# PSUM banks divided anew: four for the exponentials and one for the replicated u, instead of three and two

## The chip, the cores and the metric

The kernel runs on one core of a Trainium2 chip. A core has four computing engines with instruction streams of their own: PE (TensorE, matmuls), DVE (VectorE), ACT (ScalarE) and POOL (GpSimd); SP (SyncE) issues DMAs. They meet at semaphores alone. PSUM, where PE writes its results, has eight banks of 128 partitions by 512 float32. The metric is the device time of one execution in microseconds. Everything is float32.

## The reference

One transformer block with a Mamba layer (4 sequences of 2048 tokens, 256 channels) and a mixture of experts. The part that the change touches is the selective scan:

```
deltaA = exp(delta[..., None] * A)                 # 512 channels x 16 states
dBu = (delta * u)[..., None] * B[:, :, None, :]
h = dA_i * h + dBu_i                               # over the 2048 tokens
y = einsum('bdn,bn->bd', h, C_i)
```

Before it stand a layer norm, an input projection, a convolution over 4 tokens, silu, and the projections that give delta, B and C; behind it `y * silu(res)`, the output projection and the residual. Then comes the feed-forward part (shared expert, routing to one of seven experts), which the change doesn't touch.

## The kernel before

`build` runs five programs one after the other. `mamba_program` is the one that matters here: 16 chunks of T = 512 tokens. The 512 channels by 16 states of a chunk are cut into NSET = 16 *sets* of 32 channels. In a set the 128 partitions hold 32 channels x 4 state groups (NF), and NG = 4 state rows of 512 tokens lie beside each other, so a set has four scans of 128x512.

The work of a set s goes through all engines:

- PE replicates delta*u of the 32 channels to 128 partitions by a matmul with the constant `spread` into `u_ps` (L414, "u s" below). This is done for the ten sets in `OWN_SETS` (0 to 5, 8, 9, 12, 13). For the other six POOL does the product from a copy made by DMA.
- DVE multiplies that by B: `states_in`, L603, "SI s" below; its input is `u_ps`.
- ACT makes four exponentials into `dA` (L533), one PSUM bank each in a ring of ABANK banks.
- DVE runs the four scans (L616), which read `dA`.
- ACT copies the last column as state (L538, `save`), POOL multiplies by C (L694), PE sums the states (L424, `sum_states`), DVE gates the sum (L623).

Beside that the engines do groups of matrix work for the neighbouring chunks, placed by the table `plan` at a set: T (transposes), XS and RS (input projection), CV (convolution, four matmuls), XP, DT, DB (projections for delta, B, C) for chunk c+1, called "front", and OP (output projection) for chunk c-1, called "back". A group's result goes to one of two PSUM banks `bank0` and `bank1` and is read from there by ACT (or DVE). A float32 matmul shows in the trace as two matmul instructions, so u is two, XS or RS is four, CV eight.

There is no scheduler: every engine executes its `body` in program order. In ACT's body the four exponentials of set s come first, then `save` of set s-1, then the copies of the groups planned at s, then the exponentials of set s+1. In PE's body, at set s, `spread_u` for set s+2 comes first, then the groups planned at s, then a state sum. In DVE's body SI s+1 stands before the scans of set s, but where s+1 is a multiple of four it stands behind them (SI 4, SI 8, SI 12), and SI 5, SI 9, SI 13 follow at once, with only a gate (and behind SI 12 the layernorm statistics) in between. SI 0 and SI 1 stand together at the head of a chunk.

Two waits matter. ACT's exponential u (0 to 63 in the chunk) waits for scan u - ABANK to be done. PE's replication number i waits for the product number i-2 to be done, since `u_ps` has two halves used in turn.

Of the kernel before, what the change touches and what calls it, by code (L numbers as in the profile page):

```python
# [25 lines left out]
P = 128  # L26
# [4 lines left out]
T = 512  # L31
# [5 lines left out]
DS = 32  # L37
NSET = DI // DS
NF = P // DS
NG = STATE // NF  # L40
SPC = P // DS
RING = 8
ABANK = 3
NBANK = 2
EPS = 1e-5
BIG = 3.4028234e38
# [146 lines left out]
def mamba_program(nc, ins, t, bc_dram, x1_dram, wout_dram):  # L193
# [4 lines left out]
    with ExitStack() as ctx:  # L198
        sem = lambda n: ctx.enter_context(nc.semaphore(n))
        sb = lambda n, s: ctx.enter_context(nc.sbuf_tensor(n, s, F32))  # L200
        ps = lambda n, s: ctx.enter_context(nc.psum_tensor(n, s, F32))
# [4 lines left out]
        xpad, us, res = t["xpad"], sb("us", [P, 2, KI, T]), sb("res", [P, 2, KI, T])  # L206
# [4 lines left out]
        hs = sb("hs", [P, RING, NG, T])  # L211
        state = t["state"]
        banks = [ps(f"bank{i}", [P, T]) for i in range(NBANK)]
        y_ps, u_ps, dA = ps("y_ps", [P, T]), ps("u_ps", [P, 2, T]), ps("dA", [P, ABANK, T])

        x_loaded, stats_ready, rstd_step, shift_ready, xn_ready = sem("x_loaded"), sem("stats_ready"), sem("rstd_step"), sem("shift_ready"), sem("xn_ready")
        ln_step, hT_ready = sem("ln_step"), sem("hT_ready")
# [8 lines left out]
        dbu_own, dbu_shared, scan_done, state_saved, hc_ready = sem("dbu_own"), sem("dbu_shared"), sem("scan_done"), sem("state_saved"), sem("hc_ready")  # L226
# [4 lines left out]
        N_OWN, N_SHARED = len(OWN_SETS), len(SHARED_SETS)  # L231
# [14 lines left out]
        known = lambda c: isinstance(c, int)  # L246
# [28 lines left out]
        def bodies(eng, body):  # L275

            body(0, 0)
            body(1, 1)
            with eng.Fori(2, NCHUNK - 1 - CPB, CPB) as c:
                for i in range(CPB):  # L280
                    body(c + i if i else c, (2 + i) % CPB)
            body(NCHUNK - 2, 2)
            body(NCHUNK - 1, 3)
# [84 lines left out]
        @block.tensor  # L368
        def _(pe):
            def group(g, c, f, par=0):  # L370

                kind, j = g
                ps_ = take_bank(pe, g, c)
                if kind == "T":
                    if j == 0:
                        pe.wait_ge(xn_ready, f + 1)
                    for tt in range(TT):
                        last = nc.tensor.transpose(ps_[:, tt * P:(tt + 1) * P], xin[:, tt, j * P:(j + 1) * P], t["ident"][:])
                elif kind in ("XS", "RS"):
                    col = j * P + (DI if kind == "RS" else 0)  # L380
                    pe.wait_ge(hT_ready, KD * f + KD)
                    for k in range(KD):
                        last = nc.tensor.matmul(ps_[:, :], t["w_in"][:, k, col:col + P], hT[:, k, :], start=(k == 0), stop=(k == KD - 1))  # L383
                elif kind == "CV":
                    pe.wait_ge(xs_ready, KI * f + j + 1)
                    for k in range(KCONV):
                        last = nc.tensor.matmul(ps_[:, :], t["w_conv"][:, j, k, :], xpad[:, j, k:k + T], start=(k == 0), stop=(k == KCONV - 1))  # L387
                elif kind == "XP":
                    pe.wait_ge(us_ready, f + 1)
                    for k in range(KI):  # L390
                        last = nc.tensor.matmul(ps_[0:PROJ, :], t["w_x"][:, k, :], us[:, 1 - par, k, :], start=(k == 0), stop=(k == KI - 1))
                elif kind in ("DT", "DB"):
                    pe.wait_ge(xdbl_ready, f + 1)
                    last = nc.tensor.matmul(ps_[:, :], t["w_dt"][:, j * P:(j + 1) * P], xdbl[0:DT_ROWS, :], start=True, stop=True)  # L394
                elif kind == "OP":
                    pe.wait_ge(yg_ready, KI * c)
                    if j == 0:
                        pe.wait_ge(wout_loaded, 16 * ((c - 1) // CPB) + 16)
                    for h in range(2):
                        for k in range(KI):  # L400
                            tt = 2 * j + h
                            last = nc.tensor.matmul(ps_[:, h * D:(h + 1) * D], res[:, 1 - par, k, tt * P:(tt + 1) * P], t["w_out"][:, k, :],
                                                    start=(k == 0), stop=(k == KI - 1))
                last.then_inc(made[kind], 1)

            def spread_u(c, s, par):

                i = OWN_SETS.index(s)
                q, j = divmod(s, KI)
                if i == 0:  # L410
                    pe.wait_ge(du_ready, c + 1)
                if not (known(c) and c == 0 and i < 2):
                    pe.wait_ge(dbu_own, N_OWN * c + i - 1)
                nc.tensor.matmul(u_ps[:, i % 2, :], t["spread"][DS * q:DS * q + DS].rearrange("p f d -> p (f d)"), us[DS * q:DS * q + DS, par, j, :],  # L414
                                 start=True, stop=True, tile_position=(DS * q, 0)).then_inc(u_made, 1)

            def sum_states(c, j):

                pe.wait_ge(hc_ready, NSET * c + SPC * (j + 1))
                if not (known(c) and c == 0 and j == 0):  # L420
                    pe.wait_ge(yg_ready, KI * c + j)
                for g in range(NG):
                    for q in range(SPC):
                        last = nc.tensor.matmul(y_ps[DS * q:DS * q + DS, :], t["gather"][:], hs[:, (SPC * j + q) % RING, g, :],  # L424
                                                start=(g == 0), stop=(g == NG - 1), skip_group_check=True,
                                                tile_position=(0, DS * q))
                last.then_inc(y_ready, 1)

            def body(c, m):
                par = m % 2  # L430
                for s in range(NSET):
                    if s + 2 in OWN_SETS:
                        spread_u(c, s + 2, par)
                    for g in plan.get(s, []):
                        if has_front(c) if g in front else has_back(c):
                            group(g, c, c + 1, par)
                    if s == SUM_AT and has_back(c):
                        sum_states(c - 1, KI - 1)
                    if s > SPC and s % SPC == SUM_AT:
                        sum_states(c, s // SPC - 1)  # L440
                    if s + 2 >= NSET and has_front(c):
                        spread_u(c + 1, s + 2 - NSET, 1 - par)

            for g in front:
                group(g, None, 0, 1)
            spread_u(0, 0, 0)
            spread_u(0, 1, 0)
            bodies(pe, body)
            sum_states(NCHUNK - 1, KI - 1)
            for g in back:  # L450
                group(g, NCHUNK, None, 0)

        @block.scalar
        def _(act):
# [67 lines left out]
            def exps(c, s):  # L522
# [3 lines left out]
                for g in range(NG):  # L526
                    u = NG * s + g
                    if u >= ABANK:
                        act.wait_ge(scan_done, NG * NSET * c + u - ABANK + 1)
                    elif not (known(c) and c == 0):  # L530
                        last = max(v for v in range(NG * NSET) if v % ABANK == u)
                        act.wait_ge(scan_done, NG * NSET * (c - 1) + last + 1)
                    nc.scalar.activation(dA[:, u % ABANK, :], d_rep[:, q % 2, j, :], ACT.Exp, scale=t["a"][:, u:u + 1]).then_inc(da_ready, 1)  # L533

# [39 lines left out]
        def _(dve):  # L574
# [20 lines left out]
            def states_in(c, s, par):  # L595

                i = OWN_SETS.index(s)
                dve.wait_ge(u_made, N_OWN * c + i + 1)
                if s % KI == 0 and not (known(c) and c == 0 and s < RING):
                    dve.wait_ge(y_ready, SPC * c + (s - RING) // KI + 1)  # L600
                if s == 0:
                    dve.wait_ge(bc_loaded, 16 * 2 * NF * (c + 1))
                nc.vector.tensor_tensor(hs[:, s % RING], u_ps[:, i % 2, :].unsqueeze(1).to_broadcast([P, NG, T]),  # L603
                                        b_rep[:, par, :].rearrange("p (g t) -> p g t", g=NG), ALU.mult).then_inc(dbu_own, 1)

            def scan_set(c, s, m):
# [6 lines left out]
                for g in range(NG):  # L613
                    u = NG * s + g
                    dve.wait_ge(da_ready, NG * NSET * c + u + 1)
                    nc.vector.tensor_tensor_scan(hs[:, s % RING, g, :], dA[:, u % ABANK, :], hs[:, s % RING, g, :], state[:, u:u + 1] if m else 0.0,  # L616
                                                 ALU.mult, ALU.add).then_inc(scan_done, 1)
# [702 lines left out]
```

## Time and profile before

| | us |
|---|---|
| median of 3 runs | 3147.56 (3146.91 to 3148.33) |
| profiled execution, whole | 3146.25 |
| profiled execution, span from first to last instruction | 3144.5 |
| busy over the span: PE, DVE, POOL, ACT | 2277.3, 2028.9, 1981.0, 1363.8 |
| mean granted TensorE clock | 0.822 of full speed |

The `mamba_program` takes the span from about 60 to 2105 us; behind it stand the feed-forward programs, where PE is busy most of the time. The shares of busy time are means over both parts. What a change of the scan stage is worth is read from that stage's own waits: who stands still, for whom, and what is behind it in that engine's program order.

### The profile page before, as it was taken

Reading aid. Unit: us, or ns where it says so; the run is one execution under the profiler, and the core shown is the slowest. Engines: PE = TensorE matmul, PEld = TensorE weight load, DVE = VectorE, ACT = ScalarE, POOL = GpSimd, SP = SyncE. Lnnn points to the kernel's source line nnn. Section 1 sums busy time; section 2 is a strip of 40 time slices with the busy share of each in tenths; the row PEclk is TensorE's granted clock in tenths of the full one; section 3 lists DMA queues with packets and bytes.
Section 4 is the critical chain, followed back from the end, with each engine's and each line's share of the span. In section 5 each row is a group of like instructions: output and inputs, shape, how many; then the busy total and the mean of one; then the engine's idle time right before and its main releaser. Section 6 shows DMA issues by size and latency. Waiting matters only on the chain. (4 is left out here: it accounts for less than half of the span.)

```text
span 3144.5 us, 28848 instructions
## 1 busy us (share of the span) xinstructions
PE 2277.3 (72%) x7448; PEld 1051.1 (33%) x7449; DVE 2028.9 (65%) x2297; ACT 1363.8 (43%) x2182; POOL 1981.0 (63%) x816
## 2 busy tenths in 40 slices
PE   4768667686686677676867866437888960699998
PEld 3213223232232232232322322114555540366664
DVE  3488978879879788788798897943444441122222
ACT  1474655664655656646656556411222210122221
POOL 0298888888888888888898888950000006455553
PEclk8778788787787786877877877668999995899999
DMA  2333332432423243324324332424111110222221
GB/s 105 81 75 74 83 73 64 105 82 60 93 72 80 63 92 82 75 62 108 75 61 96 71 83 56 92 82 153 54 60 60 60 41 1 67 86 84 83 85 54
DMA packets 104208, 238.30 MB, mean 76 GB/s; under 512 B 18444, under 2 KB 72462, under 8 KB 91536
## 3 DMA queue, kind: packets, MB, share of 16 engines
q1 hardware_dynamic: 84112, 189.85, 25.0%
q0 software_dynamic: 14368, 36.00, 3.9%
q10 hardware_dynamic: 5600, 11.01, 0.9%
q8 instruction: 48, 0.79, 0.1%
q14 instruction: 80, 0.66, 0.1%
HBM read 106.10 MB, written 39.20 MB: 46 GB/s over the span
## 5 line engine op out<-in xcount | busy, mean ns | idle before, releaser
L694 POOL TENSOR_TENSOR hs<-hs,c_rep 128x2048 f32<-128x2048 f32 x256 | 1152.8, 4522 | 282.4 <-ACT state L538 282.4
L616 DVE TENSOR_TENSOR_SCAN hs<-dA,state,hs 128x512 f32<-128x512 f32 x768 | 917.9, 1261 | 206.4 <-ACT dA L533 206.4
L533 ACT ACTIVATE dA<-d_rep,a 128x512 f32<-128x512 f32 x1024 | 679.1, 686 | 468.9 <-DVE hs L616 459.3
L687 POOL TENSOR_TENSOR hs<-u_rep,b_rep 128x2048 f32<-128x2048 f32 x96 | 432.3, 4525 | 0.1
L603 DVE TENSOR_TENSOR hs<-u_ps,b_rep 128x2048 f32<-128x2048 f32 x160 | 362.3, 2273 | 5.5 <-PE u_ps L414 5.5
L394 PE MATMUL bank<-xdbl,w_dt 65*128 65x512 f32 x256 | 190.1, 874 | 242.0 <-DVE delta L592 232.7
L424 PE MATMUL y_ps<-hs,gather 128*32 128x512 f32 x2048 | 299.0, 736 | 60.6 <-POOL hs L694 60.5
L383 PE MATMUL bank<-xin,w_in 128*128 128x512 f32 x512 | 283.1, 693 | 75.5 <-ACT xdbl L491 47.6
L616 DVE TENSOR_TENSOR_SCAN hs<-dA,hs 128x512 f32<-128x512 f32 x256 | 290.5, 1201 | 71.9 <-ACT dA L533 71.9
L387 PE MATMUL bank<-xpad,w_conv 128*128 128x512 f32 x512 | 260.4, 662 | 96.0 <-DVE xres L630 94.5
L414 PE MATMUL u_ps<-us,spread 32*128 32x512 f32 x320 | 219.4, 781 | 109.2 <-POOL us L678 61.9
L788 POOL TENSOR_TENSOR rstd<-var,mhalf 128x4 f32<-128x4 f32 x16 | 16.1, 1007 | 410.8 <-DVE var L890 410.8
L1170 PE MATMUL z<-w1r,hT 128*128 x560 | 261.3, 610 | 2.6 <-issue 2.0
L1252 DVE TENSOR_TENSOR hid<-z,sg 128x512 f32<-128x512 f32 x70 | 48.4, 692 | 298.8 <-ACT sg L1230 298.8
L387 PEld LDWEIGHTS bank<-xpad,w_conv 128*128 128x128 f32 x512 | 105.7, 212 | 240.5 <-issue 129.7
L383 PEld LDWEIGHTS bank<-xin,w_in 128*128 128x128 f32 x512 | 101.5, 211 | 230.4 <-issue 123.9
L394 PEld LDWEIGHTS bank<-xdbl,w_dt 65*128 65x128 f32 x256 | 59.7, 258 | 353.5 <-DVE delta L592 254.3
L424 PEld LDWEIGHTS y_ps<-hs,gather 128*32 128x32 f32 x2048 | 70.0, 132 | 305.2 <-issue 210.2
L1137 POOL DMA_INDIRECT out<-outr,cur x70 | 71.2, 1016 | 143.4 <-DVE outr L1245 139.1
L486 ACT ACTIVATE us<-bank,cb 128x512 f32<-128x512 f32 x64 | 43.9, 686 | 245.8 <-PE bank L387 245.8
L414 PEld LDWEIGHTS u_ps<-us,spread 32*128 32x128 f32 x320 | 57.8, 218 | 255.3 <-issue 137.9
L1170 PEld LDWEIGHTS z<-w1r,hT 128*128 128x128 f32 x560 | 101.6, 191 | 120.7 <-issue 120.6
(170 smaller groups left out, 2862.2 us busy)
## 6 DMA issues: line engine op xcount, KB each, us to landing
d_rep<-delta SPq DMA_DIRECT2D x256, 256.0 KB, 4.3
u_rep<-us SPq DMA_DIRECT2D x192, 128.0 KB, 3.2
b_rep<-bc_rows SPq DMA_DIRECT2D x64, 256.0 KB, 4.5
c_rep<-bc_rows SPq DMA_DIRECT2D x64, 256.0 KB, 7.3
xin<-in_x SPq DMA_DIRECT2D x16, 512.0 KB, 3.6
xres<-in_x SPq DMA_DIRECT2D x16, 512.0 KB, 4.9
x<-xres SPq DMA_DIRECT2D x16, 512.0 KB, 3.2
x_sb<-x SPq DMA_DIRECT2D x16, 512.0 KB, 4.3
```

What stands on the lines that cost most here:

```text
L383: last = nc.tensor.matmul(ps_[:, :], t["w_in"][:, k, col:col + P], hT[:, k, :], start=(k == 0), stop=(k == KD - 1))
L387: last = nc.tensor.matmul(ps_[:, :], t["w_conv"][:, j, k, :], xpad[:, j, k:k + T], start=(k == 0), stop=(k == KCONV - 1))
L394: last = nc.tensor.matmul(ps_[:, :], t["w_dt"][:, j * P:(j + 1) * P], xdbl[0:DT_ROWS, :], start=True, stop=True)
L414: nc.tensor.matmul(u_ps[:, i % 2, :], t["spread"][DS * q:DS * q + DS].rearrange("p f d -> p (f d)"), us[DS * q:DS * q + DS, par, j, :], st ...
L424: last = nc.tensor.matmul(y_ps[DS * q:DS * q + DS, :], t["gather"][:], hs[:, (SPC * j + q) % RING, g, :], start=(g == 0), stop=(g == NG - ...
L533: nc.scalar.activation(dA[:, u % ABANK, :], d_rep[:, q % 2, j, :], ACT.Exp, scale=t["a"][:, u:u + 1]).then_inc(da_ready, 1)
L603: nc.vector.tensor_tensor(hs[:, s % RING], u_ps[:, i % 2, :].unsqueeze(1).to_broadcast([P, NG, T]), b_rep[:, par, :].rearrange("p (g t) -> ...
L616: nc.vector.tensor_tensor_scan(hs[:, s % RING, g, :], dA[:, u % ABANK, :], hs[:, s % RING, g, :], state[:, u:u + 1] if m else 0.0, ALU.mul ...
L687: nc.gpsimd.tensor_tensor(hs[:, s % RING], u_rep[:, q % 2, j - 2, :].unsqueeze(1).to_broadcast([P, NG, T]), b_rep[:, par, :].rearrange("p ...
L694: nc.gpsimd.tensor_tensor(hs[:, s % RING, :, :], hs[:, s % RING, :, :], c_rep[:, par, :].rearrange("p (g t) -> p g t", g=NG), ALU.mult).th ...
L1137: nc.gpsimd.indirect_dma_start(out, bass.IndirectOffsetOnAxis(cur[:, q, 2:3], 0), outr[:, q, :], None, bounds_check=BATCH * SEQ - 1, oob_i ...
L1170: last = nc.tensor.matmul(z[:, q % 2, half, :], hT[:, q % 2, i, :], t["w1r"][:, e, i, half * H:(half + 1) * H], start=(i == 0), stop=(i == ...
```

## The change

The eight PSUM banks are shared out differently. Before: two for the groups, one for `y_ps`, two for `u_ps`, three for `dA`. Now: two, one, one, four. `ABANK` becomes 4, so exponential u waits for scan u - 4. `u_ps` has one bank, so replication i waits for product i-1. The order of the instructions on PE, DVE, ACT and POOL is the same as before; only what they wait for differs (and a few register instructions of the sequencers that form the wait values).

```diff
-ABANK = 3
+ABANK = 4
...
-        y_ps, u_ps, dA = ps("y_ps", [P, T]), ps("u_ps", [P, 2, T]), ps("dA", [P, ABANK, T])
+        y_ps, u_ps, dA = ps("y_ps", [P, T]), ps("u_ps", [P, T]), ps("dA", [P, ABANK, T])
...
-                if not (known(c) and c == 0 and i < 2):
-                    pe.wait_ge(dbu_own, N_OWN * c + i - 1)
-                nc.tensor.matmul(u_ps[:, i % 2, :], t["spread"][DS * q:DS * q + DS].rearrange("p f d -> p (f d)"), us[DS * q:DS * q + DS, par, j, :],
+                if not (known(c) and c == 0 and i == 0):
+                    pe.wait_ge(dbu_own, N_OWN * c + i)
+                nc.tensor.matmul(u_ps[:], t["spread"][DS * q:DS * q + DS].rearrange("p f d -> p (f d)"), us[DS * q:DS * q + DS, par, j, :],
...
-                nc.vector.tensor_tensor(hs[:, s % RING], u_ps[:, i % 2, :].unsqueeze(1).to_broadcast([P, NG, T]),
+                nc.vector.tensor_tensor(hs[:, s % RING], u_ps[:].unsqueeze(1).to_broadcast([P, NG, T]),
```

## Rows read from the trace of the kernel before

**Rows 1.** Costliest groups: line engine op, shapes, count | busy us, mean ns | idle before

```profile
L616 DVE TENSOR_TENSOR_SCAN hs<-dA,state,hs 128x512 f32<-128x512 f32 x768 | 917.9, 1261 | 206.4 <-ACT dA L533 206.4
L533 ACT ACTIVATE dA<-d_rep,a 128x512 f32<-128x512 f32 x1024 | 679.1, 686 | 468.9 <-DVE hs L616 459.3
```

**Rows 2.** DVE's waits from 60 to 2130 us: for whom, total, times, longest

```profile
DVE hs L616 <- ACT dA L533: 278.2, 91, 8.1
...
DVE hs L603 <- PE u_ps L414: 5.5, 2, 4.9
```

**Rows 3.** Timeline of DVE, first half of a chunk: start, length, line, count [idle before]

```profile
1230.63 4.48 DVE L603 TENSOR_TENSOR hs<-u_ps,b_rep 128x2048 f32<-128x2048 f32 x2
...
1243.66 4.81 DVE L616 TENSOR_TENSOR_SCAN hs<-dA,state,hs 128x512 f32<-128x512 f32 x4 [1.66 <-ACT dA L533]
...
1250.57 9.50 DVE L616 TENSOR_TENSOR_SCAN hs<-dA,state,hs 128x512 f32<-128x512 f32 x8
1259.98 2.27 DVE L603 TENSOR_TENSOR hs<-u_ps,b_rep 128x2048 f32<-128x2048 f32 x1
1262.17 0.68 DVE L623 TENSOR_TENSOR res<-y_ps,res 128x512 f32<-128x512 f32 x1
...
1264.96 4.80 DVE L616 TENSOR_TENSOR_SCAN hs<-dA,state,hs 128x512 f32<-128x512 f32 x4
1271.62 4.81 DVE L616 TENSOR_TENSOR_SCAN hs<-dA,state,hs 128x512 f32<-128x512 f32 x4 [1.86 <-ACT dA L533]
...
1283.89 4.81 DVE L616 TENSOR_TENSOR_SCAN hs<-dA,state,hs 128x512 f32<-128x512 f32 x4 [6.87 <-ACT dA L533]
```

**Rows 4.** Timeline of DVE, sets 8 to 10 of the same chunk

```profile
1296.01 2.27 DVE L603 TENSOR_TENSOR hs<-u_ps,b_rep 128x2048 f32<-128x2048 f32 x1
...
1300.99 9.50 DVE L616 TENSOR_TENSOR_SCAN hs<-dA,state,hs 128x512 f32<-128x512 f32 x8
1315.37 4.81 DVE L616 TENSOR_TENSOR_SCAN hs<-dA,state,hs 128x512 f32<-128x512 f32 x4 [4.88 <-ACT dA L533]
```

**Rows 5.** Timeline of PE in the same chunk

```profile
1232.96 2.07 PE L414 MATMUL u_ps<-us,spread 32*128 32x512 f32 x2 [0.93 <-DVE hs L603]
...
1238.63 3.78 PE L383 MATMUL bank<-xin,w_in 128*128 128x512 f32 x4 [1.70 <-ACT xin L473]
...
1253.93 1.12 PE L414 MATMUL u_ps<-us,spread 32*128 32x512 f32 x2
1254.98 7.14 PE L387 MATMUL bank<-xpad,w_conv 128*128 128x512 f32 x16
1263.13 3.72 PE L402 MATMUL bank<-w_out,res 128*128 128x256 f32 x16 [1.01 <-DVE res L623]
...
1277.07 5.48 PE L387 MATMUL bank<-xpad,w_conv 128*128 128x512 f32 x8 [6.79 <-DVE xres L630]
...
1290.55 1.12 PE L414 MATMUL u_ps<-us,spread 32*128 32x512 f32 x2
1291.60 3.70 PE L383 MATMUL bank<-xin,w_in 128*128 128x512 f32 x8
1295.14 3.60 PE L391 MATMUL bank<-us,w_x 128*97 128x512 f32 x8
...
1303.74 3.00 PE L383 MATMUL bank<-xin,w_in 128*128 128x512 f32 x4 [3.29 <-ACT xdbl L491]
```

**Rows 6.** Timeline of ACT before the exponentials of set 10

```profile
1309.51 0.60 ACT L498 ACTIVATE delta<-bank 128x512 f32<-128x512 f32 x1 [0.44 <-PE bank L394]
...
1314.65 2.73 ACT L533 ACTIVATE dA<-d_rep,a 128x512 f32<-128x512 f32 x4
```

**Rows 7.** Timeline of DVE in the last chunk

```profile
2054.72 18.90 DVE L616 TENSOR_TENSOR_SCAN hs<-dA,state,hs 128x512 f32<-128x512 f32 x16
```

**Rows 8.** Windows: stretch, length, PE, PEld, DVE, ACT, POOL busy, PE clock, DMA, GB/s

```profile
1232.90:1236.90 4.00, 3.94 (x10) 2.06 (x10) 4.00 (x4) 0.57 (x1) 4.00 (x2) 0.50 0.89 187
...
1255.00:1262.10 7.10, 7.10 (x17) 2.93 (x16) 7.10 (x6) 2.20 (x4) 7.10 (x3) 1.00 0.54 111
```

## The prediction, made before the changed kernel was run

> **What bounds the kernel now.** I read the groups of instructions by line first. They show a scan stage that runs from about 120 to 2100 us: 1024 exponentials of 686 ns on ACT, 1024 scans on DVE, 768 of them at 1261 ns [rows 1], and on DVE too the products of L603, two in 4.48 us [rows 3]. DVE's waits come next. Over that stage DVE loses 278.2 us waiting for exponentials, in 91 waits, and only 5.5 us waiting for the replicated u [rows 2]. So the loop that sets the pace is DVE's: 16 chunks of some 122 us. Third come the timelines of DVE, PE and ACT in one chunk, from 1230.63 us. The reader should see that DVE's waits are not evenly spread. They stand before the scans of sets 1, 5, 6, 7, 10 and 11, 16 us or more in all per chunk, some of them in [rows 3, 4]. Each is behind one of the "front" groups: ACT's program has the copy of that group *before* the next set's exponentials, so a group that PE delivers late delays the scan. An example of the length of that link: PE ends XS0 at 1238.63 + 3.78 = 1242.41 and scan 1 starts at 1243.66, 1.25 us later; for CV3 it is 1277.07 + 5.48 = 1282.55 to 1283.89, 1.35 us [rows 3, 5]. A pair of u matmuls takes 2.07 us when PE has idled before it and 1.12 us when it has worked [rows 5].
>
> **What the fourth bank gives.** In set s, exponential 4 no longer needs scan 1 of its own set but the last scan of set s-1. It can start one scan (1.2 us) earlier, and so can the state copy and the group behind it. That helps only where ACT waits for a scan and not for PE. In set 0 ACT's fourth exponential waited 4.25 us, but the group behind it (T) was finished by PE only at about 1236.9 us, where ACT took it at 1237.1. In sets 12 to 15 DVE has no wait at all. The one place is set 9: its last exponential waits for a scan before RS3, DT0, DT1 and a silu with two table loads, and DVE waits 4.88 us behind them [rows 4]. There some 1.2 us a chunk would be gained, 19 us in all, if nothing else moved. POOL's state copies come earlier, but POOL itself doesn't bound the loop.
>
> **What the single u bank costs.** The instructions and their order stay the same on every engine. Only waits change: each replication on PE now waits for the product just before its own, not for the one before that. PE is in order, so everything behind that wait is tied to DVE. I walk the chunk from 1230.63 us. SI n is the product of set n, u n its matmul pair.
>
> *Head.* Before, u 1 is ready when SI0 ends, and u 2 starts at 1232.96. Now u 1 starts there, takes 2.07 us, SI1 runs 2.24 us behind it (half of 4.48), and u 2 starts at about 1237.4: 4.4 us later. T0, T1 and XS0 stand behind it on PE; XS0's chain sets scan 1 (DVE already waits 1.66 us for it). Scan 1 moves from 1243.66 to 1248.1. **+4.4** [rows 3, 5].
>
> *Set 2.* u 4 stands before XS3 and now waits for SI3, which ends at 1248.1 + 4.8 + 2.2 = 1255.1. PE has nothing from about 1251.9 on. u 4 then takes 2.07 us, XS3 3.00 us (the same four matmuls, after an idle time of 3.29 us, in the row at 1303.74), the link 1.25: scan 3 at 1261.5, where DVE would be there at 1259.7. **+1.7** [rows 3, 5].
>
> *Set 3, the largest.* u 5 stands before CV0 and CV1. It ran at 1253.93, well before SI4 started at 1259.98. Now it waits for SI4, which DVE does only after scan 3. From SI4's end (before: 1259.98 + 2.24 = 1262.2): 0.1 + 2.07 for u 5, 5.48 for CV0 (as CV3 after its idle time), 3.6 for CV1 (half of 7.14), 1.35 for the link, 12.6 us to scan 4. Before it was 1264.96 - 1262.2 = 2.75. **+9.8**. OP0 and CV2 now follow directly behind CV1 (3.72 + 3.60) and the link makes scan 5 start 19.9 us after SI4, before 9.4: **+0.65** more. From there on nothing is added up to scan 7: scan 6 waits for CV3, which waits for the residual of DVE behind scan 5, and that loop only shifts as a whole [rows 3, 5].
>
> *Sets 7 to 10.* u 9 ran at 1290.55, before SI8 at 1296.01. Now it waits for SI8 (end 1298.25), and RS0 and RS1 stand behind it: 0.1 + 2.07 + 3.78 (four cold matmuls, as XS0) + 1.85 (half of 3.70) + 1.25 = 9.05 us to scan 8; before 1300.99 - 1298.25 = 2.74. That is 6.3 us. XP and RS2 (3.6 + 1.9) now come directly behind: scan 9 at 14.55, before 7.5, 7.05 us. DT1 can't begin before ACT has kept RS3, behind the exponentials of set 9; with 1.5 us for DT1 and 5.1 us from its copy to the end of the silu's table loads (1309.51 to 1314.65) scan 10 starts about 24.6 us after SI8, before 17.1. For the whole stretch **+7.5**, in which the fourth bank's 1.2 us is contained, since I let set 9's exponentials run freely [rows 4 to 6].
>
> *Sets 12 to 15.* u 13 waits for SI12, but the layernorm statistics (1.8 us) and the gate (0.6 us) stand between SI12 and SI13 and cover its 2.1 us. POOL's chain shifts with the state copies of set 9, so it is no later than before against DVE. 0.
>
> Sum per chunk: 4.4 + 1.7 + 9.8 + 0.65 + 7.5 = 24.05 us. Fourteen chunks (1 to 14) have all groups: 337 us. Chunk 0 has no OP: 23.4 us. Chunk 15 has no front groups and in it DVE never waits for PE's groups [rows 7]: u 1 bare, 2.2 us, and three more of 2.2 less 0.6 us for the gate, 7.0 us. Together 367 us. From the profiled execution, span 3144.5 us and 3146.25 us in all, that is 3513 us; the median of the runs, 3147.56, is 1.3 us above the profiled one, which I neglect.
>
> **The clock.** The least certain thing is how fast PE runs behind its new idle times. The windows show the granted clock at 0.50 where PE does u 2 and T after idling and 1.00 over CV0 and CV1 [rows 8]: half speed and full speed, 1.2 and 2.4 GHz. Before my new waits PE would idle some 3 us (u 4), 2 to 5 us (u 5) and 7 us (u 9). *All at full clock:* head 4.4, set 2 nothing, set 3 6.9 + 0.65, sets 7 to 10 4.5, which is 16.5 a chunk and 251 us: 3397 us. *Cold for longer* (XS3 3.78, the state sum behind it at double length and then late for SI4 by 1.3, CV0 wholly cold at 7.2, RS1 cold): 5.7 more a chunk, about 29.8: 3599 us. I take the middle values because they are the rows of the same matmuls behind idle times of 3.3 and 6.8 us.
> The Trainium skill (TensorE: Matmul & The Clock Gate, "Part 1: The HAM clock gate") says that PE starts at half rate after idling and that activity releases it; the rows agree, and by it alone the time lies above 3397. The Trainium skill (Perfetto Trace Analysis, "Matmuls") says that independent matmul groups should rotate through PSUM banks so that reading one overlaps the next, which speaks against giving u a single bank; the price it would put on that is the sum above, and no row here shows u with one bank.
>
> **Rivals.**
> *Only the bare handshake shows.* If ACT, with its fourth bank, stays far enough ahead that PE's late groups don't reach DVE, each chunk pays only 2.2 (u 1) + 1.6 (u 5) + 1.6 (u 9): 5.4 us, in 16 chunks about 90 us: 3236 us. Against it: ACT's copies stand before the next exponentials, and four banks are one set, so a late group stops DVE after at most the set that is held. 7%.
> *Faster.* If PE's u was never a limit, for instance because u 1, 5 and 9 are back in time while DVE still has the gate to do, the fourth bank's 1.2 us per chunk at set 10 remains and is the whole effect: 19 to 22 us off, some 3127 us. It would need a u pair in under the 0.6 us that the gate covers; the shortest pair in the rows is 1.12 us. 3%.
> *The change does nothing measurable:* gains and handshakes cancel, 3147 us. 2%.
> *Cold throughout,* 3599 us as above. 10%.
> *Forecast,* 3513 us, with its clock between the ends: 78%, own range 3400 to 3570.
>
> **Numbers.** The range goes to 3580 to take in part of the cold case and stops at 3400 on the low side, as the full-clock sum is a bound. A change within 0.2% couldn't be told from none. Slower: 78 + 10 + 7, less a point that I give to faster for doubt: 94%. Same 2%, faster 3 + 1 = 4%.
>
> **What the changed profile would show.** DVE should wait before L603 for PE's u_ps some 50 to 60 times, about 2 us at the head and 1.5 at sets 5 and 9, instead of twice. The wait before scan 4, zero in most chunks now, should be some 7 us, the one before scan 8 4 to 5 us, and the chunk should repeat every 146 us. PE's idle time ended by DVE's L603 should grow from a few us a chunk to over 15. The wait before scan 6 should keep its 6.9 us. PE's matmuls L387 and L383 should grow in mean length. If scan 4 starts right behind SI5, the largest step is wrong; if CV0 and CV1 take 7.1 us together, the clock was full and the time is nearer 3400.

## The result, and the profile after

| | us |
|---|---|
| kernel before, median of 4 runs beside it | 3147.23 (3145.89 to 3148.33) |
| changed kernel, median of 4 runs | 3491.39 (3490.37 to 3493.59) |
| ratio, 95% interval | 1.1094 (1.108 to 1.1108) |
| forecast | 3513, range 3400 to 3580 |

The change costs 344 us, 10.9%. The forecast was 366 us. The profiled execution of the changed kernel spans 3489.3 us. Its costliest groups (line engine op, shapes, count | busy us, mean ns | idle before) answer to [rows 1]:

```profile
L616 DVE TENSOR_TENSOR_SCAN hs<-dA,state,hs 128x512 f32<-128x512 f32 x768 | 920.4, 1264 | 390.4 <-ACT dA L533 390.4
L533 ACT ACTIVATE dA<-d_rep,a 128x512 f32<-128x512 f32 x1024 | 660.3, 681 | 232.3 <-DVE hs L616 229.1
L414 PE MATMUL u_ps<-us,spread 32*128 32x512 f32 x320 | 262.2, 911 | 585.9 <-DVE hs L603 531.1
L603 DVE TENSOR_TENSOR hs<-u_ps,b_rep 128x2048 f32<-128x2048 f32 x160 | 364.5, 2278 | 92.2 <-PE u_ps L414 92.2
```

Nothing got more work: scans and products take as long as before. The idle times grew. ACT waits less for DVE, 229 instead of 459 us. Only some 142 us of that are the fourth bank's doing: with three banks and a single one for u (u1_ring3 below) ACT waits 371 us. Yet DVE waits more for ACT. In between stands PE, which now idles 531 us for DVE's products ahead of its replications. Before, PE's waits (whom for, us in total, times, longest) had

```profile
PE u_ps L414 <- DVE hs L603: 47.1, 18, 7.3
```

DVE's waits from 60 to 2480 us answer to [rows 2]:

```profile
DVE hs L616 <- ACT dA L533: 529.2, 148, 8.6
DVE hs L603 <- PE u_ps L414: 92.2, 51, 5.0
```

That is 251 us more for exponentials and 87 us more for u, 338 of the 344 us. Only a quarter of the loss is DVE waiting for u itself; the rest arrives by way of PE's groups and ACT.

One chunk (chunk 10) on DVE's timeline (start, length, line, count, [idle before]; scan n below is the first scan of set n), which begins at 1582.02 us as that of [rows 3, 4] does at 1230.63:

```profile
1582.02 2.28 DVE L603 TENSOR_TENSOR hs<-u_ps,b_rep 128x2048 f32<-128x2048 f32 x1
1586.46 2.29 DVE L603 TENSOR_TENSOR hs<-u_ps,b_rep 128x2048 f32<-128x2048 f32 x1 [2.16 <-PE u_ps L414]
...
1599.28 4.81 DVE L616 TENSOR_TENSOR_SCAN hs<-dA,state,hs 128x512 f32<-128x512 f32 x4 [3.63 <-ACT dA L533]
...
1611.91 4.81 DVE L616 TENSOR_TENSOR_SCAN hs<-dA,state,hs 128x512 f32<-128x512 f32 x4 [0.93 <-ACT dA L533]
1616.64 2.27 DVE L603 TENSOR_TENSOR hs<-u_ps,b_rep 128x2048 f32<-128x2048 f32 x1
...
1621.07 2.29 DVE L603 TENSOR_TENSOR hs<-u_ps,b_rep 128x2048 f32<-128x2048 f32 x1 [1.56 <-PE u_ps L414]
1631.41 4.81 DVE L616 TENSOR_TENSOR_SCAN hs<-dA,state,hs 128x512 f32<-128x512 f32 x4 [8.05 <-ACT dA L533]
...
1651.32 4.81 DVE L616 TENSOR_TENSOR_SCAN hs<-dA,state,hs 128x512 f32<-128x512 f32 x4 [7.62 <-ACT dA L533]
...
1667.66 2.29 DVE L603 TENSOR_TENSOR hs<-u_ps,b_rep 128x2048 f32<-128x2048 f32 x1 [1.56 <-PE u_ps L414]
1675.07 4.81 DVE L616 TENSOR_TENSOR_SCAN hs<-dA,state,hs 128x512 f32<-128x512 f32 x4 [5.12 <-ACT dA L533]
...
1689.71 4.81 DVE L616 TENSOR_TENSOR_SCAN hs<-dA,state,hs 128x512 f32<-128x512 f32 x4 [4.67 <-ACT dA L533]
```

The new waits are those in front of SI1, SI5 and SI9, and behind them a longer one in front of scans 1, 4 and 8 (1631.41 is scan 4, which had none before). PE's timeline of the same chunk answers to [rows 5]:

```profile
1606.33 1.12 PE L414 MATMUL u_ps<-us,spread 32*128 32x512 f32 x2 [3.61 <-DVE hs L603]
1607.38 3.29 PE L383 MATMUL bank<-xin,w_in 128*128 128x512 f32 x4
...
1618.96 2.07 PE L414 MATMUL u_ps<-us,spread 32*128 32x512 f32 x2 [4.39 <-DVE hs L603]
1620.96 9.11 PE L387 MATMUL bank<-xpad,w_conv 128*128 128x512 f32 x16
...
1665.55 2.07 PE L414 MATMUL u_ps<-us,spread 32*128 32x512 f32 x2 [7.50 <-DVE hs L603]
1667.55 6.27 PE L383 MATMUL bank<-xin,w_in 128*128 128x512 f32 x8
```

Here the mechanism stands in three pairs of rows. The replication waits for DVE, and the groups that DVE needs by way of ACT start only behind it, and slowly: CV0 and CV1 take 9.11 us where they took 7.14, RS0 and RS1 6.27 where they took 3.70. The windows of the same stretch (read as [rows 8], the clock third from the end) give the granted clock: half (0.50, 1.2 GHz) in the first 4 us of CV0 and CV1 and full (1.00, 2.4 GHz) in the rest, 0.58 over RS0 and RS1.

```profile
1621.00:1625.00 4.00, 4.00 (x6) 1.80 (x6) 2.29 (x1) 0.00 (x0) 4.00 (x2) 0.50 0.00 0
1625.00:1630.00 5.00, 5.00 (x13) 2.17 (x12) 0.00 (x0) 0.69 (x1) 3.13 (x1) 1.00 0.00 0
...
1667.50:1673.80 6.30, 6.30 (x10) 2.68 (x10) 2.29 (x1) 0.60 (x1) 4.10 (x1) 0.58 0.00 0
```

### The profile page after: what moved, and what is told of

It is laid out like the page before. It is cut to its first block and busy times, and to the rows that moved or that the text cites. A ratio compares the mean times of both kernels' runs of the same rounds, so it can differ in the third digit from the quotient of the medians.

```text
span 3489.3 us, 28860 instructions
## 1 busy us (share of the span) xinstructions
PE 2386.9 (68%) x7448; PEld 1090.3 (31%) x7449; DVE 2039.0 (58%) x2297; ACT 1348.6 (39%) x2182; POOL 1981.8 (57%) x816
## 5 line engine op out<-in xcount | busy, mean ns | idle before, releaser
L616 DVE TENSOR_TENSOR_SCAN hs<-dA,state,hs 128x512 f32<-128x512 f32 x768 | 920.4, 1264 | 390.4 <-ACT dA L533 390.4
L533 ACT ACTIVATE dA<-d_rep,a 128x512 f32<-128x512 f32 x1024 | 660.3, 681 | 232.3 <-DVE hs L616 229.1
L414 PE MATMUL u_ps<-us,spread 32*128 32x512 f32 x320 | 262.2, 911 | 585.9 <-DVE hs L603 531.1
L603 DVE TENSOR_TENSOR hs<-u_ps,b_rep 128x2048 f32<-128x2048 f32 x160 | 364.5, 2278 | 92.2 <-PE u_ps L414 92.2
L616 DVE TENSOR_TENSOR_SCAN hs<-dA,hs 128x512 f32<-128x512 f32 x256 | 291.5, 1205 | 138.8 <-ACT dA L533 138.8
L387 PE MATMUL bank<-xpad,w_conv 128*128 128x512 f32 x512 | 299.6, 745 | 96.0 <-DVE xres L630 94.5
L383 PE MATMUL bank<-xin,w_in 128*128 128x512 f32 x512 | 328.9, 796 | 28.0 <-ACT xin L473 27.2
L424 PE MATMUL y_ps<-hs,gather 128*32 128x512 f32 x2048 | 285.2, 707 | 45.2 <-POOL hs L694 45.2
L387 PEld LDWEIGHTS bank<-xpad,w_conv 128*128 128x128 f32 x512 | 120.9, 243 | 276.0 <-issue 166.0
L383 PEld LDWEIGHTS bank<-xin,w_in 128*128 128x128 f32 x512 | 121.2, 249 | 218.4 <-issue 181.1
L834 PE MATMUL y_ps<-w2s,hid 128*128 128x256 f32 x512 | 119.1, 386 | 20.5 <-DVE yg L941 18.1
```

Source lines behind the costliest of these rows:

```text
L414: nc.tensor.matmul(u_ps[:], t["spread"][DS * q:DS * q + DS].rearrange("p f d -> p (f d)"), us[DS * q:DS * q + DS, par, j, :], start=True, ...
L603: nc.vector.tensor_tensor(hs[:, s % RING], u_ps[:].unsqueeze(1).to_broadcast([P, NG, T]), b_rep[:, par, :].rearrange("p (g t) -> p g t", g ...
L834: last = nc.tensor.matmul(y_ps[:, i, :], hid[:, k, tt * P:(tt + 1) * P], w2s[:, k, :], start=(k == 0), stop=(k == KI - 1))
```

## The experiments

Each run was timed beside the kernel before. The times of the latter agree, 3146.7 to 3147.5 us.

**One part alone: a single bank for u, three for the exponentials (u1_ring3).**

```diff
-ABANK = 4
+ABANK = 3
```

> One part alone: u has a single bank, the ring of the exponentials keeps three (one bank unused). Theory A (the loss is the groups queued on PE behind the replication's new wait): all of the loss is in this part, and the fourth bank gives back little, since ACT waits for PE's groups where the time is lost: 3491 to 3515 us. Rival B (the fourth bank gives ACT a real lead and hides part of the loss): clearly slower than the changed kernel, 3540 us or more.

Measured: 3492.64 us (3490.78 to 3492.95), against the changed kernel's 3491.39. The whole loss is in the u bank. The fourth bank's worth, beside a single bank for u and in this order, is 1 us, within the spread. ACT's waits fit that: from u1_ring3 to the changed kernel its waits for DVE fall by 142 us (371 to 229) and its waits for PE's groups grow by 167 us (809 to 976). What the lead gives is spent waiting for PE.

**The order on PE: groups ahead of the replication (groups_first).** In the changed kernel's `body` of PE:

```diff
-                    if s + 2 in OWN_SETS:
-                        spread_u(c, s + 2, par)
                     for g in plan.get(s, []):
                         if has_front(c) if g in front else has_back(c):
                             group(g, c, c + 1, par)
+                    if s + 2 in OWN_SETS:
+                        spread_u(c, s + 2, par)
```

> The changed kernel with one edit: in PE's program the groups planned at a set stand ahead of the replication for set s+2, not behind it. Banks and waits are the same. Theory A: PE does the groups while it would wait for DVE, so that only the bare replication behind SI4 and SI8 and the head remain, some 6.3 us a chunk over the kernel before: 3242 us, 3215 to 3290. Rival B (the loss is the handshake itself and the slower clock of PE behind idle time, wherever the wait stands): above 3400 us.

Measured: 3275.95 us (3274.0 to 3277.36). Of 344 us, 215 are gone with the same banks and the same waits, only by what is queued behind the wait. That is theory A, and the level that rival B wanted is excluded. The clock isn't held fixed by this edit, though: in the chunk shown below CV0 and CV1 again take 7.14 us and RS0 and RS1 3.70, so a part of the 215 us is PE's speed and not its waiting. The fillers below size that part. The time lies 34 us above the value expected. DVE's timeline shows why:

```profile
1323.13 2.29 DVE L603 TENSOR_TENSOR hs<-u_ps,b_rep 128x2048 f32<-128x2048 f32 x1 [2.37 <-PE u_ps L414]
...
1345.22 2.29 DVE L603 TENSOR_TENSOR hs<-u_ps,b_rep 128x2048 f32<-128x2048 f32 x1 [0.71 <-PE u_ps L414]
...
1391.90 4.81 DVE L616 TENSOR_TENSOR_SCAN hs<-dA,state,hs 128x512 f32<-128x512 f32 x4 [2.29 <-ACT dA L533]
```

Now the replications come late in their turn: u 2 behind the slow XS0 (first row) and u 5 behind CV0 and CV1 (second row). And behind u 9, ahead of which PE idles 3.87 us, XP runs slowly (6.44 us instead of 3.60), which delays scan 9 (last row).

**One replication moved: that of set 5 (u5_late).**

```diff
-                    if s + 2 in OWN_SETS:
+                    if s + 2 in OWN_SETS and not (s == 3):
                         spread_u(c, s + 2, par)
...
+                    if s + 2 in OWN_SETS and (s == 3):
+                        spread_u(c, s + 2, par)
```

> The changed kernel, where only the replication for set 5 is moved behind CV0 and CV1. This sizes the largest step of the prediction. Theory A: scan 4 starts some 6.5 us earlier in each of 15 chunks: 3394 us, 3375 to 3415. Rival B: the pair waits for the same product and PE idles as long, 3480 to 3491 us.

Measured: 3385.90 us (3384.68 to 3386.66), 105 us less than the changed kernel, 97 expected. DVE's timeline has the trade in it (the edit adds two lines to the kernel, so L603 and L616 are L605 and L618):

```profile
1553.07 2.29 DVE L605 TENSOR_TENSOR hs<-u_ps,b_rep 128x2048 f32<-128x2048 f32 x1 [3.14 <-PE u_ps L414]
1555.27 4.80 DVE L618 TENSOR_TENSOR_SCAN hs<-dA,state,hs 128x512 f32<-128x512 f32 x4
```

SI5 waits 3.14 us instead of 1.56, and scan 4 follows at once instead of 8.05 us later. Here too the clock moved with the order: CV0 and CV1 take 7.14 us in all of chunks 1 to 14.

**One replication moved: that of set 9 (u9_late).** The same edit with `s == 7`.

> The changed kernel, where only the replication for set 9 is moved behind RS0 and RS1. Theory A: scan 8 starts some 5.1 us earlier in each of 15 chunks and XP and RS2 behind it don't take that back: 3414 us, 3400 to 3435. Rival B: 3480 to 3491 us.

Measured: 3430.08 us (3428.47 to 3434.23), 61 us less, 77 expected. The direction is right and the size is short by 16 us, about 1 us a chunk. The starts of the scans (table below) show that scan 8 gains 5.7 us, and at scan 9, behind XP and RS2, only 4.2 of it are left. PE's timeline has the reason: PE now idles 3.6 to 4.0 us ahead of u 9, and XP behind it takes 6.0 to 6.5 us in eleven of the fourteen chunks, where it took 3.60.

**The clock, with fillers (warm).** As the first experiment, and the eighth bank takes matmuls that nothing reads:

```diff
+        spare = ps("spare", [P, T])
...
+                    for _ in range({2: 2, 3: 3, 7: 6}.get(s, 0)):
+                        nc.tensor.matmul(spare[:], t["w_in"][:, 0, 0:P], t["w_in"][:, 0, 0:T], start=True, stop=True)
                     if s + 2 in OWN_SETS:
                         spread_u(c, s + 2, par)
```

> As u1_ring3, with filler matmuls on PE ahead of the waits of the replications for sets 4, 5 and 9 (2, 3 and 6 float32 matmuls of 512 columns into the eighth PSUM bank, which nothing reads), so that PE doesn't idle there. It measures the clock's part of the loss. If PE's clock stays full, u 5 with CV0 and CV1 gets shorter by 2.9 us, u 9 with RS0 and RS1 by 3.5, u 4 with XS3 by 1: some 7 us a chunk, 98 us in all against u1_ring3, about 3400 us. If the clock had no part (the idle time alone is the loss): no change against u1_ring3. If the fillers run into the waits: slower.

Measured: 3459.84 us (3457.93 to 3461.69), 33 us less than without fillers where I expected 98. PE's timeline in chunk 10 shows that the fillers didn't fill the idle time:

```profile
1591.36 2.84 PE L434 MATMUL spare<-w_in 128*128 128x512 f32 x6
1596.17 1.12 PE L415 MATMUL u_ps<-us,spread 32*128 32x512 f32 x2 [1.97 <-DVE hs L606]
1597.22 8.83 PE L388 MATMUL bank<-xpad,w_conv 128*128 128x512 f32 x16
```

Three fillers took 2.84 us and not the 3.5 I had reckoned, and left PE idle for 1.97 us. u 5 ran at full speed (1.12 us), but CV0 and CV1 behind it did not (8.83 us). The granted clock was 0.51 for 3.5 us near the start of CV0 and CV1 and 1.00 on both sides (windows, read as [rows 8]):

```profile
1596.20:1598.20 2.00, 2.00 (x5) 0.76 (x6) 1.38 (x2) 0.00 (x0) 2.00 (x1) 1.00 0.61 127
1598.20:1601.70 3.50, 3.50 (x6) 1.44 (x5) 1.42 (x1) 0.00 (x0) 3.50 (x2) 0.51 0.00 0
1601.70:1606.00 4.30, 4.30 (x12) 1.89 (x11) 0.00 (x0) 0.69 (x1) 3.30 (x1) 1.00 0.02 4
```

That isn't so in every chunk. In chunk 11 the same rows, with the same idle time, go on at full speed:

```profile
1737.89 2.84 PE L434 MATMUL spare<-w_in 128*128 128x512 f32 x6
1742.70 1.12 PE L415 MATMUL u_ps<-us,spread 32*128 32x512 f32 x2 [1.97 <-DVE hs L606]
1743.75 7.14 PE L388 MATMUL bank<-xpad,w_conv 128*128 128x512 f32 x16
```

Over chunks 1 to 14 CV0 and CV1 took 8.80 to 8.84 us in eight (idle time 1.97 to 2.22 us) and 7.14 us in six (1.71 to 1.97 us). RS0 and RS1 were slow in all of them, 5.97 to 6.62 us behind 2.05 to 2.56 us of idling. So I filled the idle time up.

**The clock, idle time filled up (warm_full).**

```diff
-                    for _ in range({2: 2, 3: 3, 7: 6}.get(s, 0)):
+                    for _ in range({2: 2, 3: 5, 7: 8}.get(s, 0)):
```

> As warm, with more fillers: 5 ahead of the wait for set 5 and 8 ahead of that for set 9, since a filler pair took 0.94 us there and left PE idle for 2.0 and 2.4 us, after which CV0 and CV1 still took 8.8 us and RS0 and RS1 6.6 us. If those idle times are what lets the clock fall, CV0 and CV1 now take 7.1 us and RS0 and RS1 3.7 us, scan 4 and scan 8 come 1.7 and 2.9 us earlier, some 4.5 us a chunk: about 3395 us. If the clock falls there for another reason (the narrow state sum and replication matmuls, say), little changes against warm: 3450 to 3465 us.

Measured: 3391.58 us (3389.22 to 3396.79). PE's timeline:

```profile
1687.78 4.56 PE L434 MATMUL spare<-w_in 128*128 128x512 f32 x10
1692.59 1.12 PE L415 MATMUL u_ps<-us,spread 32*128 32x512 f32 x2 [0.25 <-DVE hs L606]
1693.64 7.14 PE L388 MATMUL bank<-xpad,w_conv 128*128 128x512 f32 x16
```

With work in the idle time CV0 and CV1 are at 7.14 us and RS0 and RS1 at 3.70 us in all fourteen chunks, as in the kernel before, and 101 of the 345 us are gone against the same kernel without fillers. That is the clock's part at these three waits, and it comes from PE's idling ahead of them. The other 244 us are waiting for the most part, but not alone: at the head u 1 still takes 2.07 us behind its idle time, and no filler stands there.

**What a bank of the ring is worth (u2_ring2).** The kernel before with `ABANK = 2`; u keeps two banks.

> The kernel before with a ring of two banks for the exponentials in place of three; u keeps its two. It shows what a bank of the ring is worth. Theory A (the ring hardly matters since ACT waits for PE's groups): the copies behind a set's exponentials come one scan, 1.2 us, later at three to five places a chunk: 3210 to 3240 us. Rival B (the ring is what lets ACT run ahead, a bank of it is worth several us a chunk): 3300 us or more.

Measured: 3239.56 us (3237.61 to 3244.28), 93 us slower. It lies at the upper end of theory A's range; rival B's 3300 isn't reached. The means below show the steps of 1 to 2 us that theory A wanted, at scans 1, 7, 10 and 11. From two banks to three the ring gains 93 us, from three to four 1 us (beside a single u bank). The fourth bank with two banks for u wasn't tried: the eight banks don't hold it.

**The loop at scan 6 (swap_before).** The kernel before with one swap in `plan`:

```diff
-                4: [("OP", 0), ("CV", 2)], 5: [("CV", 3), ("OP", 1)],
+                4: [("CV", 2), ("OP", 0)], 5: [("CV", 3), ("OP", 1)],
```

> The kernel before with one swap in the table of groups: at set 4 CV2 stands ahead of OP0. By the alternation CV3 then takes the bank that ACT empties, not the one that DVE's residual behind scan 5 empties. It tests the reading that scan 6's wait of 6.9 us is that loop. Theory A: scan 6 and scan 7 come 8 to 9 us earlier and the chunk gets shorter by about 8 us: 3035 us, 3000 to 3070. Rival C (POOL, with 105 us of work a chunk, or scan 10's table loads take the gain back): 3100 to 3147 us.

Measured: 3027.72 us (3027.07 to 3032.74), ratio 0.9623 (0.9607 to 0.9639) against the kernel before: 3.8% faster than it. This is the version that beats both. DVE's timeline around scan 6:

```profile
1197.28 9.50 DVE L616 TENSOR_TENSOR_SCAN hs<-dA,state,hs 128x512 f32<-128x512 f32 x8
1206.69 0.66 DVE L630 TENSOR_TENSOR xres<-bank,xres 128x512 f32<-128x512 f32 x1
1207.28 4.80 DVE L616 TENSOR_TENSOR_SCAN hs<-dA,state,hs 128x512 f32<-128x512 f32 x4
1211.99 0.66 DVE L630 TENSOR_TENSOR xres<-bank,xres 128x512 f32<-128x512 f32 x1
1214.66 4.81 DVE L616 TENSOR_TENSOR_SCAN hs<-dA,state,hs 128x512 f32<-128x512 f32 x4 [2.01 <-ACT dA L533]
```

The wait of 6.87 us of [rows 3] is gone, and that of 1.86 us in front of scan 5 too (scans 4 and 5 stand in one row of eight). CV3 now takes the bank that ACT empties, and the output projection waits for the residual instead, where nobody hurries. POOL didn't take the gain back.

**Both edits on the changed kernel (swap_groups_first).**

> The changed kernel with both edits: groups ahead of the replications on PE, and CV2 ahead of OP0 at set 4. If the two are independent, it comes out at groups_first less what the swap gives to the kernel before, 3100 to 3150 us if those are 3242 and -110; it shows whether the bank division could pay once the order suits it.

Measured: 3112.02 us (3109.45 to 3112.63). It is 35 us or 1.1% faster than the kernel before (ratio 0.9887, 0.9871 to 0.9904), and 84 us slower than the swap alone. So the best order that I tried with this division of the banks is 84 us behind the best with the old one; what the fourth bank has of it in this order wasn't separated. The swap gave 164 us here and 119 us there: the two edits aren't independent. Against its counterpart with the old division the chunk is 5.1 us longer here (against swap_before) and 8.6 us in groups_first (against the kernel before; table below). 1.3 of the 3.5 us between them are there at scan 4, most of the rest comes by scan 9: PE idles 2.0 us or less ahead of u 9 here and 3.6 to 4.0 there, and XP behind it takes 3.67 us in six chunks and 5.37 in eight here, where it takes 5.8 to 6.5 there.

**Where in the chunk the time is.** From DVE's timelines I took, for chunks 1 to 14, when each set's first scan starts after the chunk's first product, and subtracted the same of the kernel before (means, us; worked out from the timelines, not a view of the profile):

```
                     scan 1   scan 3   scan 4   scan 6   scan 8   scan 9   next chunk
changed kernel        +4.4     +5.6    +15.6    +16.3    +23.0    +23.5    +22.9
u1_ring3              +4.4     +5.5    +15.2    +15.8    +22.6    +23.1    +22.9
u5_late               +4.4     +5.7     +9.0     +9.1    +15.9    +16.4    +15.9
u9_late               +4.4     +5.9    +15.6    +16.2    +17.3    +19.3    +18.8
groups_first          +3.1     +3.1     +6.1     +5.7     +7.0     +9.2     +8.6
warm                  +4.5     +5.0    +12.8    +13.4    +20.1    +20.6    +20.5
warm_full             +4.5     +4.9    +11.7    +11.7    +15.1    +15.5    +15.4
u2_ring2              +1.1     +1.5     +1.8     +1.7     +2.9     +3.2     +6.4
swap_before           +0.1     +0.4     +0.8     -8.3     -8.3     -8.3     -8.5
swap_groups_first     +2.9     +2.9     +5.6     -3.7     -3.5     -2.7     -3.4
```

## Why the prediction was right, and where it was off

*The mechanism.* The prediction said that the replication's new wait ties PE's groups to DVE and that the time comes out as late exponentials. The profile after shows it, and groups_first, u5_late and u9_late show that the queue behind the wait is what costs: the same wait with other work behind it is up to 215 us cheaper, by less waiting and a faster PE together.

*Head.* Forecast 4.4, measured 4.4 (scan 1).

*Set 2.* Forecast 1.7, measured 1.2 as a mean. The forecast had u 4 cold, 2.07 us, since PE idles before it. That was so in one of the fourteen chunks (chunk 1, behind 3.69 us). In ten others u 4 ran warm (1.12 us) behind 3.37 to 3.77 us of idling, and XS3 behind it was slow, 2.94 to 3.43 us; in chunks 5, 9 and 13 PE didn't idle there and XS3 took 1.98 us. So "2.07 us when PE has idled" is no rule, and the term was too high by half a microsecond.

*Set 3.* Forecast 9.8, measured 15.6 - 5.6 = 10.0. The row at 1618.96 has u 5 cold, and CV0 and CV1 together take 9.11 us, where I had 5.48 + 3.6 = 9.1. From scan 4 to scan 5 I forecast 0.65 and the means show 0.2; up to scan 6 it was 0.7, since CV3 took 6.23 us in the chunk shown, not 5.48. That part of "nothing is added" was off by half a microsecond a chunk.

*Sets 7 to 10.* Forecast 7.5 in all: 6.3 at scan 8 and 7.05 at scan 9. Measured from scan 7 on 7.0, 7.4, and 6.8 at the end of the chunk, the last being the one overestimate here. I had the part from scan 9 to scan 10 longer than before by another 0.5 us, and it is shorter by the same: DVE waits 4.67 us there, 4.88 before.

*Sum.* 22.9 us a chunk were measured, 24.05 forecast. Over 14 chunks that is 16 of the 22 us by which the forecast was too high; chunk 0 took 20.4 and not 23.4 us more, and the last one 6.5 of my 7.0 by its last scans. Outside the scans the changed kernel takes 3.9 us less behind the last one and 0.9 us more ahead of the first product, which I had left out. So the sum came out close because most of its terms did, and not because large errors cancelled: no term was off by more than 0.7 us a chunk (sets 7 to 10).

*The fourth bank.* I counted nothing for it beyond 1.2 us a chunk at set 9's exponentials. In all it is worth 1 us (u1_ring3), and that step doesn't show: with three banks the length of the chunk is the same. The waits that it was to remove, ACT's for scans in the middle of set 9's exponentials (0.7 to 0.9 us a chunk before), are 0.07 to 0.23 us with three banks: those exponentials come later now, behind XP and RS2, when the scans are done.

*The clock.* My sum "all at full clock", 3397 us, isn't quite that: its 4.4 us at the head have a cold pair in them. It can be compared with warm_full, which is at full clock behind u 4, u 5 and u 9 and cold at the head: 3391.58. What the clock added is 101 us measured, 116 by my sum (3513 - 3397). The step that had least support held in its size.

*Rivals.* The bare handshake (3236 us) would have needed scans that don't wait for late groups; they do, 148 times instead of 91. "Faster" and "no change" fell with it. Cold throughout (3599 us) did not happen: CV1 and XP ran warm.

*What I said the profile would show:* 51 waits for u against 50 to 60 forecast; 8.05 us before scan 4 (7); 5.12 before scan 8 (4 to 5); a chunk of 146.8 us as the mean of chunks 1 to 14 (146). PE's idle time ended by DVE's products went from 47 to 531 us, over 30 us a chunk ("over 15"), and the matmuls L387 and L383 grew in the mean from 662 to 745 ns and from 693 to 796 ns. Scan 6's wait grew to 7.6 us, where I had said it would keep its 6.9.

## What to carry to other kernels

A buffer's depth has to be judged by what its *writer* has queued behind the wait for it. The replication itself is 1 to 2 us, but on an in-order engine everything behind it is tied to the reader, and its cost came out four times as large as the reader's own wait for it. Walk one period, engine by engine, from the timeline's rows, before giving a buffer away, and look first at who waits for whom: of ACT's 459 us of waiting for DVE the fourth bank took a good part away and the time didn't move, at least beside a single bank for u. The same reading of two alternating banks (who empties the one that the next group needs?) found a swap of two entries that is worth 119 us.

## What the runs showed of the hardware

The granted clock can fall *behind* a short idle time that the next matmuls still crossed at full speed, and the length of the idle time doesn't tell whether it will. In the run with three fillers PE idled 1.97 us, did u 5 at full speed (1.12 us) and then took 8.83 us for what takes 7.14; one chunk later the same rows with the same 1.97 us were followed by 7.14 us. In the changed kernel u 4 was cold behind 3.69 us in chunk 1 and warm behind 3.77 us in chunk 14. With 0.51 us of idling or less ahead of u 5 (warm_full) CV0 and CV1 took 7.14 us in all of chunks 1 to 14. So a warm first matmul behind a gap isn't evidence that the gap was free, and one chunk isn't enough to judge a gap by.

A float32 matmul of 512 columns shows as two instructions and takes 0.89 to 0.94 us in a row at full clock, fillers (sixteen instructions in 7.13 us, four in 1.88) and real ones (sixteen of CV0 and CV1 in 7.14 us) alike. I had reckoned three fillers at 3.5 us, near the mean of real ones, which has the slow ones in it, and that left the gap. Idle time filled by count has to be measured and not reckoned.

Four exponentials in a row took 2.73 us with three banks [rows 6] and take less with four. ACT's timeline in the changed kernel:

```profile
1637.59 2.51 ACT L533 ACTIVATE dA<-d_rep,a 128x512 f32<-128x512 f32 x4
```

In the changed kernel 183 of 192 such rows took 2.51 to 2.53 us. With one bank for u and three for the exponentials (u1_ring3) none of 129 took less than 2.65 us, and the median is 2.73, as before. So the shorter rows go with the fourth bank. Why a row of four is 0.22 us shorter with it wasn't tested.
